# The scan's C slice asked for ahead of the B slice in SyncE's queue

## The reference

```python
xdbl = xm @ W_xp
dtr, Bm, Cm = jnp.split(xdbl, [DTR, DTR + DS], axis=-1)
dt = jax.nn.softplus(dtr @ W_dt + b_dt)
A = -jnp.exp(A_log)
def step(hst, inp):
    dt_t, B_t, C_t, x_t = inp
    dA = jnp.exp(dt_t[:, :, None] * A)
    hst = hst * dA + (dt_t * x_t)[:, :, None] * B_t[:, None, :]
    y = jnp.einsum('bds,bs->bd', hst, C_t)
    return (hst, y)
...
y = jnp.transpose(ys, (1, 0, 2)) + xm * D_param
```

## Time and profile before

| | us |
|---|---|
| median of 3 runs | 5344.82 (5313.51 to 5346.1) |
| the profiled execution | 5308.23 |
| its span | 5306.5 |
| DVE busy in it | 4653.1 (88%) |
| PE busy in it | 4408.0 (83%) |
| POOL busy in it | 4054.0 (76%) |
| ACT busy in it | 3277.8 (62%) |

### The profile page before, as it was taken

The page is one execution under the profiler, slowest core; times in us unless marked ns, Lnnn a source line. Parts: engine busy times, 40 slices in busy tenths (PEclk is TensorE's granted clock), DMA queues, the critical chain, the costliest instruction groups (busy, mean ns, idle before and its releaser), DMA issues.

```text
span 5306.5 us, 54840 instructions
## 1 busy us (share of the span) xinstructions
PE 4408.0 (83%) x16792; PEld 2421.4 (46%) x16792; DVE 4653.1 (88%) x4552; ACT 3277.8 (62%) x5574; POOL 4054.0 (76%) x2840
## 2 busy tenths in 40 slices
PE   3677898888888888888888888888889888888765
PEld 1244454444444444444454444445444444444433
DVE  2885899999999899999999999999999999997573
ACT  2564566666766666676666667666666666665352
POOL 1874787878878788887878788787878888786472
PEclk8788899999999999998989999899999999998777
DMA  4763666767766676676767677676767767675362
GB/s 147 236 218 126 201 232 233 238 222 240 256 219 232 221 243 230 236 261 217 237 223 233 230 241 261 217 240 216 241 233 240 246 233 250 214 242 184 105 220 64
DMA packets 355050, 1164.53 MB, mean 219 GB/s; under 512 B 39347, under 2 KB 79330, under 8 KB 354758
## 3 DMA queue, kind: packets, MB, share of 16 engines
q1 hardware_dynamic: 310598, 1106.42, 61.9%
q10 hardware_dynamic: 44160, 54.60, 3.4%
HBM read 1140.78 MB, written 20.10 MB: 219 GB/s over the span
## 4 chain that ended last, share of the span: by engine, by line
DVE 41%; PE 28%; issue 12%; ACT 9%; DMA 5%; POOL 4%; SPq 1%; ACTq 0%; DVEq 0%; POOLq 0%
DVE hw L1234 20%; DVE ps L1220 8%; PE ps L1121 5%; PE ps L1472 5%; PE ps L1499 4%; PE ps L893 3%; PE ps L1334 3%; DVE mx L1592 3%; ACT pts L1567 2%; DMA bs<-bc_scratch 2%; ACT da L1170 2%; POOL hw L1252 2%; DMA xhat<-in_x 2%; DVE stats L819 1%; DVE u L1073 1%
## 5 line engine op out<-in xcount | busy, mean ns | idle before, releaser
L1252 POOL TENSOR_TENSOR hw<-hw,cs 128x1024 f32<-128x1024 f32 x1024 | 2414.3, 2358 | 664.2 <-DVE hw L1234 620.4
L1234 DVE TENSOR_TENSOR_SCAN hw<-da,ps 128x1024 f32<-128x1024 f32 x1024 | 2335.1, 2280 | 29.0 <-PE ps L1121 6.2
L1170 ACT ACTIVATE da<-dt,a_neg 128x510 f32<-128x510 f32 x2048 | 1326.1, 710 | 233.8 <-DVE hw L1234 230.1
L1259 POOL TENSOR_TENSOR hw<-hw 128x512 f32<-128x512 f32 x1024 | 1298.5, 1268 | 69.5
L1220 DVE TENSOR_TENSOR ps<-ps,bs 128x1024 f32<-128x1024 f32 x1024 | 1256.6, 1227 | 59.4 <-DMA bs<-bc_scratch 18.8
L1121 PE MATMUL ps<-hw,ident 128*128 128x512 f32 x2048 | 1128.9, 662 | 116.1 <-POOL hw L1259 115.8
L1121 PEld LDWEIGHTS ps<-hw,ident 128*128 128x128 f32 x2048 | 403.2, 209 | 574.8 <-issue 320.2
L893 PE MATMUL ps<-hT,w_in 128*128 128x512 f32 x1024 | 531.4, 650 | 86.4 <-DVE dt L1081 69.4
L1567 ACT ACTIVATE pts<-ps 128x512 f32<-128x512 f32 x512 | 280.2, 593 | 381.4 <-PE ps L1499 381.3
L1592 DVE TENSOR_REDUCE mx<-ps 128x2 f32<-128x512 f32 x512 | 329.7, 683 | 151.6 <-PE ps L1472 151.6
L770 ACT ACT_TABLE_LOAD x321 | 411.8, 1283 | 28.9 <-DVE x_c L1782 23.3
(11 more groups left out here) (180 smaller groups left out, 5344.8 us busy)
## 6 DMA issues: line engine op xcount, KB each, us to landing
bs<-bc_scratch SPq DMA_DIRECT2D x1024, 512.0 KB, 5.0
cs<-bc_scratch SPq DMA_DIRECT2D x1024, 512.0 KB, 3.8
taps<-taps_scratch SPq DMA_DIRECT2D x32, 512.0 KB, 6.3
xhat<-in_x ACTq DMA_DIRECT2D x16, 512.0 KB, 5.2
gate<-gates_scratch ACTq DMA_DIRECT2D x64, 128.0 KB, 4.3
x_b<-in_x ACTq DMA_DIRECT2D x16, 512.0 KB, 7.1
x_scratch<-x_b ACTq DMA_DIRECT2D x16, 512.0 KB, 3.7
x_c<-x_scratch ACTq DMA_DIRECT2D x16, 512.0 KB, 4.8
```

The costliest lines, as they stand in the source:

```text
L1170: ins = nc.scalar.activation(da[q % (AHEAD + 1)][:, k, :, 1:S], dt_[:, c, :].rearrange("p (b s) -> p b s", b=GB)[:, :, 1:S], ACT.Exp, scal ...
L1234: nc.vector.tensor_tensor_scan(tile[:, :, :].rearrange("p n t -> p (n t)"), da[s % (AHEAD + 1)][:, :, :, :].rearrange("p n b s -> p (n b s)"),
L1252: nc.gpsimd.tensor_tensor(tile[:, :, :], tile[:, :, :], cs[s % C_RING][:, :, :], ALU.mult)\
L1259: nc.gpsimd.tensor_tensor(tile[:, 0, :], tile[:, 0, :], tile[:, 1, :], ALU.add)\
```

## The change

In `scan_sync` the two requests of one place change their order: the C slice of step s-1 is asked for first, then the B slice of step s. Waits, buffers, places and the code of all other engines stay.

```diff
             for s in range(STEPS):
                 yield s - B_RING + 1 + AT["load"]
-                slice_in(bs[s % B_RING], s, B_RING, 0, "dbx", b_in)
                 if s:
                     slice_in(cs[(s - 1) % C_RING], s - 1, C_RING, NS, "mul", c_in)
+                slice_in(bs[s % B_RING], s, B_RING, 0, "dbx", b_in)
```

## The result

The changed kernel takes 5566.3 us (median of 4 runs, 5553.8 to 5570.4) against 5345.5 us: the two medians lie 221 us apart. The forecast was +87 us; its direction was right and its size was not. The profiled execution has a span of 5552.1 us, 245.6 us over the one before. The execution profiled before, 5308 us, is 37 us under its median.

What follows compares the result with a forecast made beforehand. VectorE (DVE) was taken as first bound, TensorE and ScalarE replacing it over a third of the time. Of 154 us new waits 97 stay, less 10 gained: +87 on the median 5344.8, 5432 us; range 5365 to 5525.

Steps and rivals of the forecast that it cites:

- B(s) takes the slot that B(s+1) had: SyncE's queue: 992 of 1024 B slices are asked for one POOL step later, landing about when the next B landed.
- The three kinds of places: Around s = 13 and at the two sorts of scan start, DVE newly waits 3.1, 2.9 and 1.6 us on the mean.
- the subtraction: Cost at a place: landing of the next B slice less the start of the dbx needing this one.
- All other steps together give some 2 us for a pair of scans, when a delay already taken is subtracted: Steps outside s = 13 and scan starts, mostly s = 15, 22, 25, 30: some 2 us of DVE waits per scan pair.
- the 130 to 250 named as the sign: Changed profile: DVE's wait for B slices was to grow from 18.8 us to 130 to 250.
- 0.63 of it stays: At the kernel's end: PE and ACT hold 37% of the chain and forgive that share, so 97 us of waits stay.
- the predicted 154 us: Sum of new DVE waits for B over all scans: 16 x (3.1 + 2.9 + 1.6 + 2.0).
- the stated range: Time of the whole changed kernel: 5365 to 5525 us.
- the 10: Microseconds taken as gained at scan starts from B(0) landing sooner, out of a possible 27.
- Busy times of all engines stay: Sign in the changed profile: no engine's busy time changes.
- The gain at B(0): Scan starts: B(0) lands sooner because B(1) and B(2) are asked for later; 10 us taken, between 0 and 27.
- Nothing absorbed, or it feeds back: Rival: waits fall where DVE is packed, and late scans delay mul and the next B; 5499 to 5523 us, chance 0.15.

Runs made afterwards that it cites:

- e4: Kernel before, with the C request ahead of B at all steps except 0 to 5, 13 and 17 to 22; ratio 1.0186.
- e9: Kernel before, with the C request ahead of B at steps 12 to 16 alone; ratio 1.0145.
- e10: Kernel before, with the C request ahead of B at steps 13 and 17 to 22 alone; ratio 1.0294.
- e1: Kernel before, with the C request ahead of B at step 13 alone, in all 32 scans; ratio 1.0119.
- e2: Kernel before, with the C request ahead of B at steps 17 to 22 alone; ratio 1.0207.
- e5: Kernel before, B still asked for ahead of C, but waiting first for the same mul as C; ratio 1.0248.
- e7: Changed kernel, with each B request made one POOL step later still, waiting for mul(s-2); 6430 us, one run.
- e3: Kernel before, with the C request ahead of B at steps 0 to 5 alone, the scan starts; ratio 1.0137.
- e11: Kernel before, with the C request ahead of B at steps 23 to 31 alone; ratio 1.0135.
- e12: Kernel before, with the C request ahead of B at steps 6 to 31, all but the scan starts; ratio 1.0358.
- e6: Changed kernel with three C buffers in place of two, q and v attention weights sharing the k tile; ratio 1.0024 to the kernel before.
- e8: Kernel before, old order, with 28 of 32 taps loads moved from behind B(0) to behind B(10); 5316.9 us, ratio 0.9969.

## Why the prediction was wrong, by its own steps

**"B(s) takes the slot that B(s+1) had": right.** SyncE's waits for dbx fell from 272 to 15 us, and those for mul rose from 3775 to 4226 us. Of the 992 B requests, 977 stand 0.36 or 0.37 us behind a C request and none more than 0.67.

**The three kinds of places: right, to a few us.** At s = 13 the subtraction gave 3.1 us for a scan, 50 us in all; DVE's waits there, added up dbx by dbx, are 52. At the starts (s = 1 to 5) it gave 2.9 us on the even places and 1.6 on the odd ones, 72 us in all; they are 71. That the sum fits so well is in part luck: it is 46 forecast and 40 measured on the even places, 26 and 30 on the odd ones. These sizes came from rows of the kernel before alone, by landing of the next slice less start of the dbx.

**"All other steps together give some 2 us for a pair of scans, when a delay already taken is subtracted": this step failed.** That made 32 us; measured are 140. The same subtraction at s = 19 of the scan above, from a row of before, is right again: the slice in B(20)'s slot landed at 2904.45 and dbx(19) had begun at 2901.77, 2.7 us, against the 2.86 measured; over the 16 such scans it gives 38 us against 39. I had struck it out as covered by the 4.5 us of s = 13. Cover is real, but it lasts only until POOL, by waiting for DVE, is as late as DVE: dbx(14) right behind s = 13 was covered (e4, e9), dbx(19) was not (the 126.22 us of both engines at s = 16; e10 against e1 and e2). s = 19 is 39 of the 108 us that are missing. The others are mostly at s = 15, 22, 25, 28, 30 and 31, with 9 to 15 us each; these I did not follow one by one. With waits of 52 + 71 + 140 and 17 at B(0) as before, the sum is 280, over the 130 to 250 named as the sign.

**"0.63 of it stays": this step failed too.** 229 of 260.5 us stay, 0.88; by the spans of the two profiled executions it is 245.6 of 260.5, 0.94. In e1, e5 and e7 it is about all (64 of 60, 132 of 122, 1095 of 1118), in e3, e9, e11 and e12 0.8 to 1, in e2 and e10 1.2, in e4 0.62, in e6 0.3 (13 of 41); with intervals of 9 to 28 us either way, most of the waits stay, and no one share is fixed. The chain's share of PE and ACT was read as time in which DVE may be late. The forecast had DVE's waits for PE shrink by 30 to 60 us; they grew by 27, from 412.6 to 439.5, and in the traces of e1 to e4 and e9 to e12 they are 425 to 459. Only the waits for ACT (27 us) and for other transfers (12 us) gave way. Why those for TensorE did not is argued and not shown: part of its work waits for DVE's own results (its matmuls L1472 waited 97 us for DVE's maxima), and its clock was lower. A chain tells who was last, not how late the others may be. With the measured waits and the 0.63 the forecast would have been 5500; with the predicted 154 us and 0.88 it would have been 5470. Both lie inside the stated range; it took both steps to leave it. (The 5390 to 5460 given for a third to three quarters of the 154 do not follow either: less the 10 it is 5386 to 5450.)

**"Busy times of all engines stay": not for TensorE,** which was busy 92 us longer, at a lower granted clock. The forecast has no term for it; what it is worth is open, and the 25 us above are an estimate.

**The gain at B(0): sooner, but not for the reason given, and without effect on the waits.** B(0) landed in 4.8 us on the mean in place of 5.5 (the 6.7 of the earlier trace rows, on which the gain was sized, is not typical), POOL's wait for C fell from 35.3 to 17.2 us; DVE's wait at s = 0 stayed 17 us in all. The forecast put the gain down to B(1) and B(2) close behind B(0). But two things changed there: B(1) goes out 2.6 us behind B(0) in place of 1.6 (medians), and C(31) of the scan before goes out 3.1 us ahead of it in place of 1.2. With B(1) later alone (e3) B(0) took 5.43 us, with C(31) earlier and B(1) not later (e4, e11, e12) 5.2 to 5.3, with neither (the kernel before, e1, e2, e9, e10) 5.5 to 5.9. Neither alone gives the 0.7 us, and how the two act together is open. By the Trainium skill ("DMA: Bandwidth & Descriptors", section "Queues, rings and completion order") descriptors of one ring are taken in order, from which I drew that nothing asked for later could hold B(0) up. e8 doesn't bear that out: the requests ahead of B(0) are as before and taps no longer follows 0.36 us behind it, and it landed 0.56 us sooner.

**The rivals.** "Nothing absorbed, or it feeds back" was the nearest, with 5499 to 5523 us. It took the 154 us as given, so it was short as well. The feedback it names, a late scan that makes mul and the next B late, is what the 126.22 us show.

## What to carry to other kernels

In a queue that works in order, a request pays for the wait of whatever stands ahead of it: put the one whose buffer is free first, and look not at how long the requests take but at which wait each stands behind. What a later request costs can be read from the profile of before, place by place, as the landing of the slice in the new slot less the start of its user; strike out a place as covered only if the engine that releases the request has not, by waiting for the delayed engine in between, become as late itself. If the bound engine gets new waits, count most of them: here 0.88, and from 0.6 to all of them in the parts. The share that other engines hold of the last chain does not tell how much they give back.

## What the runs showed that I had not expected

- A transfer was slowed by a request made right behind it on the same queue: B(0), 5.51 us on the mean with taps 0.4 us behind it, 4.95 us without (e8). Moving B(1) from 1.6 to 3.5 us behind it did far less (e3, 5.43).
- Of two slices of 512 KB asked for 0.36 us apart the first landed in 3.7 to 4.2 us and the second in 4.9 to 5.1 (medians of five kernels), whichever of the two it is (e5 against the kernel before).
- TensorE, which the change does not touch, was busy 92 us longer for the same matmuls, at a mean granted clock of 0.895 in place of 0.905.
